# Overflow work of a third gathered in one place behind the upper projection, and the overflow tokens of the next expert transposed under a condition

## The chip, the cores and the metric

The kernel runs on one core of one Trainium2 chip. The metric is the device time in microseconds (us) of one execution. It was 2561.84 us before the change (median of 3 runs, 2560.95 to 2563.5). The granted TensorE clock of the profiled execution was 0.987 of full speed over the whole span.

## The reference, cut to what matters

The program is a cross attention, a self attention and a mixture of experts over 1024 tokens of 512 features. The change touches only the experts:

```python
NUM_EXPERTS, TOPK, FFN, CAPACITY = 64, 8, 1536, 160
gates = softmax(x @ wg.T); w_topk, idx_topk = top_k(gates, TOPK)      # 8 experts a token
# tokens sorted by expert; at most CAPACITY = 160 of them are kept for each expert
h = einsum('ech,efh->ecf', buf, expert_w1)       # gate and upper halves, 512 -> 2 x 1536
x1, x2 = split(h, 2)
out = einsum('ecf,ehf->ech', x1 * silu(x2), expert_w2)                # 1536 -> 512
result = x + shared_out + scatter_add(out * gate weight)
```

A mean expert gets 128 tokens (1024 x 8 / 64). Up to 160 count, so an expert has 128 regular tokens and up to 32 "overflow" tokens.

## The kernel before

**Tiling.** The 64 experts are worked off in order, each in three thirds of the hidden width (NB = 3, so n runs from 0 to 191; b = n % 3, e = n // 3). A third has three weight units of 1 MB: GATE, UPPER and DOWN. A unit lands in one of 10 slots (8 in `ring`, 2 in `e_more`). ScalarE rounds it to fp32r (`high`, line 1269, into e_WH), VectorE takes the rest (`low`, line 1348, into e_WL); both have 5 places (HELD), and a place is free again once TensorE has used the unit that was there. TensorE multiplies three times (high x high, high x low, low x high) for each of four slices, 12 matmuls of 128x512 a unit.

**The regular work of a third on TensorE**, in this order: `gates_of(n)` (12 matmuls, lines 1457 to 1459), `uppers_of(n)` (12, the same lines), `turn(n-1)` (4 fp32 transposes of the product of the third before, line 1507), `down(n-2)` (12 matmuls, lines 1535 to 1537).

**The overflow work.** The 32 overflow tokens are laid out as four column strips of 32: `over(n)` (line 1488) is 64 small fp32 matmuls with an output of 32x128, straight from the raw GATE and UPPER units; `over_turn(n-1)` (line 1498) is one fp32 transpose of 128x128; `over_down(n-2)` (line 1520) is 32 small matmuls from the raw DOWN unit. `narrow[e]` is 1 if expert e has at most 128 tokens and so no overflow; TensorE reads it into a register and skips `over` and `over_down` then. This text calls such an expert narrow, and the others wide. The overflow work stands in three places of a third: `over_turn` and `over` between `gates_of` and `uppers_of`, `over_down` between `turn` and `down`. With b = 0, `over_turn` runs outside the condition.

**The tokens of the next expert.** In the thirds with b = 1, between `gates_of` and `uppers_of`, `turn_tokens(e+1)` makes four fp32 transposes of the regular tokens (line 1445) and one of the overflow tokens (line 1448), always. It waits for the gather, for the copies out of the PSUM banks (`xel_done`, `xeo_done`), and, only ahead of the last transpose, for `gto_done`. ScalarE copies both out (lines 1299 and 1306), VectorE makes the low half (1370).

**The order on the other engines** is written out by hand and is the same for every third. ScalarE, step n: [b = 2: the weighing of the expert before, 1313 and 1314], `high(UPPER, n+1)`, `silu(n)` (1277), [b = 1: the token copies], `high(DOWN, n-1)`, `silu_over(n)` (1284), `high(GATE, n+2)`, `copy_turned(n-1)` (1291 and 1292). VectorE, step n: `low(UPPER, n+1)`, [b = 1: low tokens], `low(DOWN, n-1)`, `product(n)` (1356), `product_over(n)` (1363), `low(GATE, n+2)`, `turned_low(n-1)` (1376). Each of these runs for narrow experts too. SyncE's queue issues the loads (line 1257) in the order of use, each when the unit that was in its slot 10 loads earlier is used up: for GATE and UPPER of third n at `u_done` (the upper projection of n is done), for DOWN at `d_done`. GpSimd gathers tokens and adds results into DRAM.

Of the kernel before, what the change touches and what calls it, by code (L numbers as in the profile page):

```python
# [14 lines left out]
P = 128  # L15
# [4 lines left out]
G = D // P  # L20
# [3 lines left out]
NE = 64  # L24
# [91 lines left out]
def program(nc, x, ctx_k, ctx_v, wq, wk, wv, wo, bq, bk, bv, bo, wg, shared, experts, out):  # L116
    root = ExitStack()
    with root:
# [1070 lines left out]
        with ExitStack() as st:  # L1189
# [61 lines left out]
            @block.sync  # L1251
            def _(sp):
                for i in range(RING, 3 * NP):
                    if i >= R:
                        kind, n = ORDER[i - R]
                        sp.wait_ge(d_done if kind == DOWN else u_done, n + 1)
                    sp.dma_start(unit(i), source(i)).then_inc(unit_in[i % R], 16)

            @block.scalar
            def _(act):  # L1260
                def high(kind, n):

                    i = place(kind, n)
                    act.wait_ge(unit_in[i % R], 16 * (i // R + 1))
                    nth = NTH[kind, n]
                    if nth >= HELD:
                        was, m = SPLITS[nth - HELD]
                        act.wait_ge(consumed[was], m + 1)
                    act.activation(WH[:, nth % HELD, :], unit(i), ACT.Copy).then_inc(hi_done, 1)  # L1269

                def silu(n):
                    act.wait_ge(g_done, n + 1)
                    if n == 0:
                        act.wait_ge(so_out, 32)
                    if n >= 2:
                        act.wait_ge(gf_done, n - 1)
                    act.activation(SL[n % 2], gate_ps, ACT.Silu).then_inc(silu_done, 1)  # L1277

                def silu_over(n):

                    act.wait_ge(u_done, n + 1)
                    if n >= 1:
                        act.wait_ge(gfo_done, n)
                    act.activation(SLo[:, :], over_ps[:, 0:P], ACT.Silu).then_inc(slo_done, 1)  # L1284

                def copy_turned(n):

                    act.wait_ge(t_done, n + 1)
                    if n >= 2:
                        act.wait_ge(d_done, n - 1)  # L1290
                    act.activation(GTh[:, n % 2, :, :], turn_ps.rearrange("p (j n) -> p j n", j=G), ACT.Copy).then_inc(gt_done, 1)
                    act.activation(GTo[:, n % 2, :, :], overturn_ps.rearrange("p (j n) -> p j n", j=G), ACT.Copy).then_inc(gto_done, 1)

                def tokens_high(e):

                    act.wait_ge(xe_psum, e + 1)
                    if e >= 2:
                        act.wait_ge(u_done, NB * (e - 1))
                    act.activation(XEh[:, e % 2, :, :], token_ps.rearrange("p (k n) -> p k n", k=G), ACT.Copy).then_inc(xeh_done, 1)

                def tokens_over(e):

                    act.wait_ge(xe_psum, e + 1)
                    if e >= 2:
                        act.wait_ge(u_done, NB * (e - 1))
                    act.activation(XEo[:, e % 2, :, :], overtoken_ps.rearrange("p (k n) -> p k n", k=G), ACT.Copy).then_inc(xeo_done, 1)

                def weigh(e):

                    act.wait_ge(d_done, NB * e + NB)  # L1310
                    if e >= 1:
                        act.wait_ge(added, 32 * e)
                    act.activation(Y, down_ps, ACT.Copy, scale=gates[:, e, 0:1]).then_inc(y_ready, 1)
                    act.activation(Y2, overdown_ps, ACT.Copy, scale=gates[:, e, 1:2]).then_inc(y2_ready, 1)  # L1314

                high(GATE, 0)
                tokens_high(0)
                high(UPPER, 0)
                tokens_over(0)
                high(GATE, 1)  # L1320
                for n in range(NP):
                    e, b = n // NB, n % NB
                    if b == 2 and e >= 1:
                        weigh(e - 1)
                    if n + 1 < NP:
                        high(UPPER, n + 1)
                    silu(n)
                    if b == 1 and e + 1 < NE:
                        tokens_high(e + 1)
                        tokens_over(e + 1)  # L1330
                    if n >= 1:
                        high(DOWN, n - 1)
                    silu_over(n)
                    if n + 2 < NP:
                        high(GATE, n + 2)
                    if n >= 1:
                        copy_turned(n - 1)
                high(DOWN, NP - 1)
                copy_turned(NP - 1)
                weigh(NE - 1)  # L1340

            @block.vector
            def _(dve):
# [14 lines left out]
                def product_over(n):  # L1358

                    dve.wait_ge(slo_done, n + 1)  # L1360
                    if n >= 1:
                        dve.wait_ge(t_done, n)
                    dve.tensor_tensor(GFo[:, :], SLo[:, :], over_ps[:, P:2 * P], ALU.mult).then_inc(gfo_done, 1)

                def tokens_low(e):

                    dve.wait_ge(xeh_done, e + 1)
                    if e >= 2:
                        dve.wait_ge(u_done, NB * (e - 1))
                    dve.tensor_tensor(XEl[:, e % 2, :, :], token_ps.rearrange("p (k n) -> p k n", k=G), XEh[:, e % 2, :, :],  # L1370
                                      ALU.subtract).then_inc(xel_done, 1)
# [10 lines left out]
                low(GATE, 1)  # L1382
                for n in range(NP):
                    e, b = n // NB, n % NB
                    if n + 1 < NP:
                        low(UPPER, n + 1)
                    if b == 1 and e + 1 < NE:
                        tokens_low(e + 1)
                    if n >= 1:
                        low(DOWN, n - 1)  # L1390
                    product(n)
                    product_over(n)
                    if n + 2 < NP:
                        low(GATE, n + 2)
                    if n >= 1:
                        turned_low(n - 1)
                low(DOWN, NP - 1)
# [37 lines left out]

            @block.tensor
            def _(pe):
                def turn_tokens(e):

                    pe.wait_ge(gathered[e % 2], 32 * (e // 2 + 1))  # L1440
                    if e >= 1:
                        pe.wait_ge(xel_done, e)
                        pe.wait_ge(xeo_done, e)
                    for k in range(G):
                        pe.transpose(token_ps[:, k * P:(k + 1) * P], XG[:, e % 2, k * P:(k + 1) * P], ident[:, :])  # L1445
                    if e >= 2:
                        pe.wait_ge(gto_done, NB * (e - 1))
                    pe.transpose(overtoken_ps, XO[:, e % 2, :], ident[:, :]).then_inc(xe_psum, 1)  # L1448

                def project(dst, kind, n, done):  # L1450

# [18 lines left out]
                def uppers_of(n):  # L1470

                    if n >= 1:
                        pe.wait_ge(gf_done, n)
                    project(up_ps, UPPER, n, u_done)
# [17 lines left out]
                def over_turn(n):  # L1492

                    pe.wait_ge(gfo_done, n + 1)
                    if n >= 1:
                        pe.wait_ge(gto_done, n)
                    pe.wait_ge(xeo_done, min((n - 1) // NB + 2, NE))
                    pe.transpose(overturn_ps, GFo[:, :], ident[:, :])  # L1498

                def turn(n):  # L1500
# [36 lines left out]
                        last = pe.matmul(down_ps, l, wh, start=False, stop=(b == NB - 1 and j == G - 1))  # L1537
                    last.then_inc(d_done, 1)

                turn_tokens(0)  # L1540
                before = None
                for e in range(NE):
                    now = pe.value_load(narrow[0:1, e:e + 1], min_val=0, max_val=1)
                    for b in range(NB):
                        n = NB * e + b
                        gates_of(n)
                        if b == 0 and n >= 1:
                            over_turn(n - 1)
                        with pe.If(now < 1):
                            if b >= 1:  # L1550
                                over_turn(n - 1)
                            over(n)
                        if b == 1 and e + 1 < NE:
                            turn_tokens(e + 1)
                        uppers_of(n)
                        if n >= 1:
                            turn(n - 1)
                        if n >= 2:
                            with pe.If((now if b >= 2 else before) < 1):
                                over_down(n - 2)  # L1560
                            down(n - 2)
                    before = now
                over_turn(NP - 1)
# [63 lines left out]
```

## Time and profile before

| | |
|---|---|
| median of 3 runs | 2561.84 us (2560.95 to 2563.5) |
| profiled execution, own time | 2563.15 us |
| its span | 2561.4 us |
| PE (TensorE) busy | 2469.9 us, 96% |
| VectorE busy | 1982.8 us, 77% |
| ScalarE busy | 1674.0 us, 65% |
| GpSimd busy | 624.8 us, 24% |
| HBM over the span | 277 GB/s |
| the experts' part | from 601.6 us to the end |

Busy times are sums over the whole span; the first 600 us are the attentions, the routing and the shared expert. PE matmuls overlap in the profile (each is shown with 0.39 us but they start 0.23 us apart), so their starts have to be read, not their durations. "PEld" is TensorE's loading of the held operand.

### The profile page before, as it was taken

Reading aid. Unit: us, or ns where it says so; the run is one execution under the profiler, and the core shown is the slowest. Engines: PE = TensorE matmul, PEld = TensorE weight load, DVE = VectorE, ACT = ScalarE, POOL = GpSimd, SP = SyncE. Lnnn points to the kernel's source line nnn. Section 1 sums busy time; section 2 is a strip of 40 time slices with the busy share of each in tenths; the row PEclk is TensorE's granted clock in tenths of the full one; section 3 lists DMA queues with packets and bytes.
Section 4 is the critical chain, followed back from the end, with each engine's and each line's share of the span. In section 5 each row is a group of like instructions: output and inputs, shape, how many; then the busy total and the mean of one; then the engine's idle time right before and its main releaser. Section 6 shows DMA issues by size and latency. Waiting matters only on the chain.

```text
span 2561.4 us, 53432 instructions
## 1 busy us (share of the span) xinstructions
PE 2469.9 (96%) x21954; PEld 1969.7 (77%) x21954; DVE 1982.8 (77%) x1878; ACT 1674.0 (65%) x2107; POOL 624.8 (24%) x541
## 2 busy tenths in 40 slices
PE   6877989998999999999999999999999999999998
PEld 5763557776888888888888888888888888888886
DVE  6863457665799889998878988988778877867785
ACT  5641233334688788887767878877667767756774
POOL 3410020101233322422222332233212222222221
PEclk9988999998999999999999999999999999999999
DMA  6770022235899999999988999999889888877894
GB/s 202 221 218 0 2 108 106 97 153 197 288 381 384 343 351 384 378 377 328 355 300 317 365 347 353 384 349 346 291 304 322 319 299 314 323 282 269 317 361 131
DMA packets 128524, 714.96 MB, mean 279 GB/s; under 512 B 15488, under 2 KB 23808, under 8 KB 52416
## 3 DMA queue, kind: packets, MB, share of 16 engines
q1 hardware_dynamic: 102048, 665.96, 68.2%
q0 software_dynamic: 26144, 44.06, 8.6%
q8 instruction: 272, 4.46, 0.7%
q14 instruction: 60, 0.49, 0.1%
HBM read 684.46 MB, written 25.49 MB: 277 GB/s over the span
## 4 chain that ended last, share of the span: by engine, by line
PE 76%; DVE 0%; POOL 0%; issue 0%; ACT 0%; ACTq 0%; POOLq 0%; DVEq 0%
PE ps L1457 14%; PE ps L1459 14%; PE ps L1458 14%; PE ps L1535 7%; PE ps L1537 7%; PE ps L1536 7%; PE ps L1488 5%; PE ps L1507 3%; PE ps L1520 3%; PE ps L1445 1%; PE ps L1498 0%; PE ps L1448 0%; DVE e_WL L1348 0%; ACT e_WH L1269 0%; POOL out_rows L1419 0%
## 5 line engine op out<-in xcount | busy, mean ns | idle before, releaser
L1348 DVE TENSOR_TENSOR e_WL<-ring,e_WH 128x2048 fp32r<-128x2048 f32 x462 | 1057.3, 2289 | 227.7 <-ACT e_WH L1269 223.6
L1269 ACT ACTIVATE e_WH<-ring 128x2048 fp32r<-128x2048 f32 x462 | 883.5, 1913 | 115.8 <-PE ps L1537 98.8
L1457 PE MATMUL ps<-e_WH,e_XEh 128*128 128x512 f32 x1536 | 614.9, 400 | 3.6 <-DVE e_XEl L1370 3.6
L1459 PE MATMUL ps<-e_WH,e_XEl 128*128 128x512 f32 x1536 | 602.0, 392 | 0.0
L1458 PE MATMUL ps<-e_WL,e_XEh 128*128 128x512 f32 x1536 | 599.4, 390 | 0.0
L1407 POOL TENSOR_TENSOR e_tick<-e_tick 128x1 f32<-128x1 f32 x126 | 132.3, 1050 | 1337.8 <-ACT X L1314 1136.7
L1457 PEld LDWEIGHTS ps<-e_WH,e_XEh 128*128 128x128 f32 x1536 | 289.0, 188 | 72.3 <-issue 9.1
L1459 PEld LDWEIGHTS ps<-e_WH,e_XEl 128*128 128x128 f32 x1536 | 288.8, 188 | 62.8
L1458 PEld LDWEIGHTS ps<-e_WL,e_XEh 128*128 128x128 f32 x1536 | 289.4, 188 | 56.2
L1535 PE MATMUL ps<-e_WH,e_GTh 128*128 128x512 f32 x768 | 319.5, 416 | 0.4 <-issue 0.3
L1348 DVE TENSOR_TENSOR e_WL<-e_more,e_WH 128x2048 fp32r<-128x2048 f32 x114 | 260.8, 2289 | 53.9 <-ACT e_WH L1269 52.9
L1537 PE MATMUL ps<-e_WH,e_GTl 128*128 128x512 f32 x768 | 300.5, 391 | 0.0
L1536 PE MATMUL ps<-e_WL,e_GTh 128*128 128x512 f32 x768 | 299.9, 390 | 0.0
L1269 ACT ACTIVATE e_WH<-e_more 128x2048 fp32r<-128x2048 f32 x114 | 218.1, 1913 | 23.8 <-PE ps L1537 23.7
L1277 ACT ACTIVATE X<-ps 128x512 f32<-128x512 f32 x192 | 114.9, 599 | 97.6 <-PE ps L1459 97.6
L1535 PEld LDWEIGHTS ps<-e_WH,e_GTh 128*128 128x128 f32 x768 | 144.3, 188 | 39.1 <-issue 15.2
L1537 PEld LDWEIGHTS ps<-e_WH,e_GTl 128*128 128x128 f32 x768 | 144.2, 188 | 33.1
L1421 POOL DMA_INDIRECT out_rows<-X,lists x64 | 159.0, 2484 | 19.5 <-issue 19.5
L1536 PEld LDWEIGHTS ps<-e_WL,e_GTh 128*128 128x128 f32 x768 | 144.8, 189 | 24.2
L1284 ACT ACTIVATE e_SLo<-ps 128x128 f32<-128x128 f32 x192 | 53.2, 277 | 163.5 <-PE ps L1459 163.5
L1356 DVE TENSOR_TENSOR X<-X,ps 128x512 f32<-128x512 f32 x192 | 130.9, 682 | 15.8 <-PE ps L1459 15.8
L1376 DVE TENSOR_TENSOR e_GTl<-ps,e_GTh 128x512 fp32r<-128x512 f32 x192 | 131.1, 683 | 0.0
(207 smaller groups left out, 3269.7 us busy)
## 6 DMA issues: line engine op xcount, KB each, us to landing
ring<-in_experts SPq DMA_DIRECT2D x462, 1024.0 KB, 7.9
e_more<-in_experts SPq DMA_DIRECT2D x114, 1024.0 KB, 7.8
ring<-in_shared SPq DMA_DIRECT2D x12, 1536.0 KB, 6.3
a_K<-in_ctx_k SPq DMA_DIRECT2D x32, 514.0 KB, 5.2
a_V<-in_ctx_v SPq DMA_DIRECT2D x32, 384.0 KB
a_V<-in_ctx_v SPq DMA_DIRECT2D x32, 130.0 KB
X<-in_x SPq DMA_DIRECT2D x4, 512.0 KB, 5.3
xn_scratch<-ring SPq DMA_DIRECT2D x1, 2048.0 KB, 7.4
```

The source lines that it names most:

```text
L1269: act.activation(WH[:, nth % HELD, :], unit(i), ACT.Copy).then_inc(hi_done, 1)
L1348: dve.tensor_tensor(WL[:, at, :], unit(place(kind, n)), WH[:, at, :], ALU.subtract).then_inc(lo_done, 1)
L1356: dve.tensor_tensor(GF[n % 2], SL[n % 2], up_ps, ALU.mult).then_inc(gf_done, 1)
L1376: dve.tensor_tensor(GTl[:, n % 2, :, :], turn_ps.rearrange("p (j n) -> p j n", j=G), GTh[:, n % 2, :, :], ALU.subtract).then_inc(gtl_done, 1)
L1407: pool.tensor_tensor(tick[:, :], tick[:, :], tick[:, :], ALU.add).then_inc(ticked, 1)
L1421: pool.indirect_dma_start(out4, bass.IndirectOffsetOnAxis(lists[:, 1, e, 1:2], 0), Y2, None, compute_op=ALU.add).then_inc(added, 16)
L1457: pe.matmul(dst, h, wh, start=(k == 0), stop=False)
L1458: pe.matmul(dst, h, wl, start=False, stop=False)
L1459: last = pe.matmul(dst, l, wh, start=False, stop=(k == G - 1))
L1535: pe.matmul(down_ps, h, wh, start=(b == 0 and j == 0), stop=False)
L1536: pe.matmul(down_ps, h, wl, start=False, stop=False)
L1537: last = pe.matmul(down_ps, l, wh, start=False, stop=(b == NB - 1 and j == G - 1))
```

## The change

On TensorE, `turn_tokens(e+1)` moves to the start of the third (ahead of `gates_of`), the overflow transpose in it comes first and only if the next expert is wide. `over(n)`, `over_down(n-2)` and `over_turn(n-1)` stand together between `uppers_of(n)` and `turn(n-1)`, and all of them are conditional. The register for the next expert is read one expert ahead. The raw GATE and UPPER units are now read after `uppers_of`, so their slots are given back at `t_done` (the turn behind the overflow work) and not at `u_done`. On ScalarE and VectorE the token work goes to the start of the step, and `silu_over(n)` and `product_over(n)` behind the work on GATE of n+2; `silu_over` waits for `t_done`.

```diff
@@ block.sync
-                        sp.wait_ge(d_done if kind == DOWN else u_done, n + 1)
+                        if kind == DOWN:
+                            sp.wait_ge(d_done, n + 1)
+                        elif n >= 1:
+                            sp.wait_ge(t_done, n)
+                        else:
+                            sp.wait_ge(u_done, 1)
@@ block.scalar, silu_over
-                    act.wait_ge(u_done, n + 1)
+                    if n >= 1:
+                        act.wait_ge(t_done, n)
+                    else:
+                        act.wait_ge(u_done, 1)
@@ block.scalar, the steps
+                    if b == 1 and e + 1 < NE:
+                        tokens_high(e + 1)
+                        tokens_over(e + 1)
                     if n + 1 < NP:
                         high(UPPER, n + 1)
                     silu(n)
-                    if b == 1 and e + 1 < NE:
-                        tokens_high(e + 1)
-                        tokens_over(e + 1)
                     if n >= 1:
                         high(DOWN, n - 1)
-                    silu_over(n)
                     if n + 2 < NP:
                         high(GATE, n + 2)
+                    silu_over(n)
@@ block.vector, the steps
+                    if b == 1 and e + 1 < NE:
+                        tokens_low(e + 1)
                     if n + 1 < NP:
                         low(UPPER, n + 1)
-                    if b == 1 and e + 1 < NE:
-                        tokens_low(e + 1)
...
-                    product_over(n)
                     if n + 2 < NP:
                         low(GATE, n + 2)
+                    product_over(n)
@@ block.tensor, turn_tokens
-                    for k in range(G):
-                        pe.transpose(token_ps[:, k * P:(k + 1) * P], XG[:, e % 2, k * P:(k + 1) * P], ident[:, :])
                     if e >= 2:
                         pe.wait_ge(gto_done, NB * (e - 1))
-                    pe.transpose(overtoken_ps, XO[:, e % 2, :], ident[:, :]).then_inc(xe_psum, 1)
+                    with pe.If(alone < 1):
+                        pe.transpose(overtoken_ps, XO[:, e % 2, :], ident[:, :])
+                    for k in range(G):
+                        last = pe.transpose(token_ps[:, k * P:(k + 1) * P], XG[:, e % 2, k * P:(k + 1) * P], ident[:, :])
+                    last.then_inc(xe_psum, 1)
@@ block.tensor, over_turn
-                    pe.wait_ge(xeo_done, min((n - 1) // NB + 2, NE))
+                    pe.wait_ge(xeo_done, min(n // NB + 2, NE))
@@ block.tensor, the thirds
+                        if b == 1 and e + 1 < NE:
+                            turn_tokens(e + 1, after)
                         gates_of(n)
-                        if b == 0 and n >= 1:
-                            over_turn(n - 1)
-                        with pe.If(now < 1):
-                            if b >= 1:
-                                over_turn(n - 1)
-                            over(n)
-                        if b == 1 and e + 1 < NE:
-                            turn_tokens(e + 1)
+                        if n == 0:
+                            with pe.If(now < 1):
+                                over(n)
                         uppers_of(n)
+                        if b < 2 and n >= 2:
+                            with pe.If(before < 1):
+                                over_down(n - 2)
+                                if b == 0:
+                                    over_turn(n - 1)
                         if n >= 1:
+                            with pe.If(now < 1):
+                                over(n)
+                                if b == 2:
+                                    over_down(n - 2)
+                                if b >= 1:
+                                    over_turn(n - 1)
                             turn(n - 1)
                         if n >= 2:
-                            with pe.If((now if b >= 2 else before) < 1):
-                                over_down(n - 2)
                             down(n - 2)
```

## Rows read from the trace of the kernel before

**Rows 1.** The page: busy time by engine, and the chain that ended last.
```profile
PE 2469.9 (96%) x21954; PEld 1969.7 (77%) x21954; DVE 1982.8 (77%) x1878; ACT 1674.0 (65%) x2107; POOL 624.8 (24%) x541
...
PE 76%; DVE 0%; POOL 0%; issue 0%; ACT 0%; ACTq 0%; POOLq 0%; DVEq 0%
```

**Rows 2.** The waits of the whole span: us in total, times, longest.
```profile
PEld ps L1488 <- issue: 19.8, 68, 0.4
```

**Rows 3.** By line, count; ns min/median/max, first and last start.
```profile
L1488 PE MATMUL ps<-ring,e_XEo x3616: 272/273/298, 611.5 to 2505.7; 128*32 128x128 f32 x191
...
L1488 PE MATMUL ps<-e_more,e_XEo x800: 272/273/298, 640.9 to 2493.4; 128*32 128x128 f32 x160
...
L1498 PE MATMUL ps<-ident,e_GFo x110: 270/270/328, 619.1 to 2541.6; 128*128 128x128 f32 x110
...
L1448 PE MATMUL ps<-ident,XO x64: 272/272/421, 602.5 to 2495.0; 128*128 128x128 f32 x64
```

**Rows 4.** PE's timeline, two narrow thirds: start us, us, line, count.
```profile
809.63 0.39 PE L1457 MATMUL ps<-e_WH,e_XEh 128*128 128x512 f32 x1
...
812.35 0.27 PE L1498 MATMUL ps<-ident,e_GFo 128*128 128x128 f32 x1
...
815.23 0.60 PE L1507 MATMUL ps<-ident,X 128*128 128x128 f32 x4
...
818.43 0.39 PE L1457 MATMUL ps<-e_WH,e_XEh 128*128 128x512 f32 x1
...
821.16 0.60 PE L1445 MATMUL ps<-ident,XG 128*128 128x128 f32 x4
...
821.62 0.49 PE L1457 MATMUL ps<-e_WH,e_XEh 128*128 128x512 f32 x1
...
824.50 0.60 PE L1507 MATMUL ps<-ident,X 128*128 128x128 f32 x4
```

**Rows 5.** PE's timeline, a wide third: one transpose, over, upper projection, turn.
```profile
1504.05 0.27 PE L1498 MATMUL ps<-ident,e_GFo 128*128 128x128 f32 x1
1504.24 1.08 PE L1488 MATMUL ps<-ring,e_XEo 128*32 128x128 f32 x32
1505.14 1.06 PE L1488 MATMUL ps<-e_more,e_XEo 128*32 128x128 f32 x32
1506.13 0.50 PE L1457 MATMUL ps<-e_WH,e_XEh 128*128 128x512 f32 x1
...
1508.99 0.60 PE L1507 MATMUL ps<-ident,X 128*128 128x128 f32 x4
```

**Rows 6.** PE's timeline, over followed by the token transposes.
```profile
1515.12 1.96 PE L1488 MATMUL ps<-ring,e_XEo 128*32 128x128 f32 x64
1517.00 0.66 PE L1445 MATMUL ps<-ident,XG 128*128 128x128 f32 x4
...
1517.52 0.48 PE L1457 MATMUL ps<-e_WH,e_XEh 128*128 128x512 f32 x1
```

**Rows 7.** PE's timeline, turn, over_down and down.
```profile
1531.24 0.60 PE L1507 MATMUL ps<-ident,X 128*128 128x128 f32 x4
1531.77 1.08 PE L1520 MATMUL ps<-ring,e_GTo 128*32 128x128 f32 x32
1532.78 0.50 PE L1535 MATMUL ps<-e_WH,e_GTh 128*128 128x512 f32 x1
```

**Rows 8.** PEld's timeline behind a skipped over_down.
```profile
1119.56 0.19 PEld L1535 LDWEIGHTS ps<-e_WH,e_GTh 128*128 128x128 f32 x1 [0.34 <-issue]
```

**Rows 9.** ScalarE's timeline in the first narrow third of rows 4.
```profile
815.43 0.28 ACT L1284 ACTIVATE e_SLo<-ps 128x128 f32<-128x128 f32 x1 [0.47 <-PE ps L1459]
...
817.88 0.28 ACT L1292 ACTIVATE e_GTo<-ps 128x128 f32<-128x128 f32 x1
```

**Rows 10.** The loads at line 1257, and a stretch of narrow experts (busy us, clock, DMA share, GB/s).
```profile
DMA to landing us min/median/max: 4.6/7.9/12.3
...
716.00:860.00 144.00, 144.00 (x681) 118.70 (x680) 134.15 (x104) 122.98 (x135) 49.04 (x33) 1.00 1.01 382
```

More of the change, by code:

```diff
@@ L1437, in _, with turn_tokens @@
             def _(pe):
-                def turn_tokens(e):
+                def turn_tokens(e, alone):
                     pe.wait_ge(gathered[e % 2], 32 * (e // 2 + 1))
@@ L1538, in down @@
                     last.then_inc(d_done, 1)
-                turn_tokens(0)
-                before = None
+                now = pe.value_load(narrow[0:1, 0:1], min_val=0, max_val=1)
+                turn_tokens(0, now)
+                before = after = None
                 for e in range(NE):
-                    now = pe.value_load(narrow[0:1, e:e + 1], min_val=0, max_val=1)
+                    if e >= 1:
+                        now = after
+                    if e + 1 < NE:
+                        after = pe.value_load(narrow[0:1, e + 1:e + 2], min_val=0, max_val=1)
                     for b in range(NB):
                         n = NB * e + b
+                        if b == 1 and e + 1 < NE:
+                            turn_tokens(e + 1, after)
                         gates_of(n)
-                        if b == 0 and n >= 1:
-                            over_turn(n - 1)
-                        with pe.If(now < 1):
-                            if b >= 1:
-                                over_turn(n - 1)
-                            over(n)
-                        if b == 1 and e + 1 < NE:
-                            turn_tokens(e + 1)
-                        uppers_of(n)
-                        if n >= 1:
+                        if n == 0:
+                            with pe.If(now < 1):
+                                over(n)
+                        uppers_of(n)
+                        if b < 2 and n >= 2:
[3 more added lines that the diff above has]
+                                    over_turn(n - 1)
+                        if n >= 1:
+                            with pe.If(now < 1):
[4 more added lines that the diff above has]
+                                    over_turn(n - 1)
                             turn(n - 1)
                         if n >= 2:
-                            with pe.If((now if b >= 2 else before) < 1):
-                                over_down(n - 2)
                             down(n - 2)
```

## The prediction

> **What bounds the kernel now.** I read the page first: PE is busy 96% of the span and holds 76% of the chain that ended last, with nothing from another engine above 0% [rows 1]. Then the waits: of TensorE's there is hardly one for another engine; what remains is "issue", such as 19.8 us ahead of the overflow loads [rows 2]. Then PE's timeline, third by third, by starts, since shown durations overlap. The expert part is a train without holes: 12 matmuls of 512 columns take 2.72 to 2.73 us (809.63 to 812.35 [rows 4]), and the other engines run behind with idle time of their own. So the time is the sum of what TensorE issues, and the change is priced there; the other engines count only where the new order makes TensorE wait.
>
> **Prices on TensorE.**
> - A regular block of 12: 2.725 us.
> - A turn and the down block behind it: 815.23 to 818.43, 3.20 us [rows 4]. With 2.725 for the block that leaves .475 for four transposes, some .107 each and .04 for the return to big matmuls. One transpose alone (over_turn of a narrow expert, skipped over behind it) costs 815.23 - 812.35 - 2.725 = .155 [rows 4].
> - Five token transposes alone, 821.16 to 821.62, .46, and the block behind 2.88: .61 in all [rows 4].
> - 32 small matmuls: .90 (1504.24 to 1505.14) [rows 5].
> - Going into the small ones: transpose to over 1504.05 to 1504.24, .19 instead of .107, so .09 [rows 5]; four transposes to over_down .53 instead of .43, so .10 [rows 7]. Take .10. An entry straight from a big matmul isn't in these rows; between 0 and .25 (a whole matmul pitch), I take .10.
> - Leaving them: the second 32 take .99 and the block behind 2.86 instead of 2.725, so .22 into big matmuls [rows 5]. Into transposes: over takes 1.88 (.08 more than 1.80) and the five cost .52 instead of .46 [rows 6], so .14.
>
> So each excursion into the small matmuls costs .24 to .32 us besides its work. Why: PEld sits idle with "issue" 68 times, a total of 19.8 us, just ahead of line 1488 [rows 2], which is .29 each; the first small load doesn't begin under the matmul before it, as other loads do. The Trainium skill, TensorEngine Tiling (Array Packing), Key Properties, says that changing the tiling mode, not merely the tile, drains the engine; by that rule two runs of the same mode back to back pay once. The rows have no over beside an over_down, so that they merge is what I infer: between free (the ring half and the e_more half of rows 5 stand .90 apart) and the full .32. I take free, since both use the same 128x32 form.
>
> **How often.** Line 1488 ran 3616 + 800 = 4416 times [rows 3], 64 a third: 69 thirds, 23 wide experts, 41 narrow ones. Line 1498 ran 110 times: 46 within wide experts, 64 outside any condition [rows 3]. By the timeline the wide ones are 0, 1, 9, 19, 23, 24, 26, 31, 38, 41, 42, 43, 45, 47, 49, 50, 52, 54 to 58 and 62. Of the 63 boundaries 9 are wide-wide, 13 narrow-wide, 14 wide-narrow, 27 narrow-narrow.
>
> **The sum, by kind of third** (base without extras: three blocks 8.175 + .475 = 8.65; entry .10, exit into transposes .14):
> - b = 2, wide. Before: .19 + 1.89 + .135 for transpose, over and exit, .10 + .90 + .235 for over_down (its .11 tail and .125 in the down block): 12.10, read as 12.06. After: 8.65 + .10 + 2.70 + .14 + .107 = 11.70. Saves .36 x 23 = 8.3.
> - b = 0, wide-wide: over_down and over_turn in one condition, over in the next, so two excursions: 8.65 + .10 + .90 + .14 + .107 + .10 + 1.80 + .14 = 11.94 against 12.06. Saves .12 x 9 = 1.1.
> - b = 0, narrow-wide: 10.69 against 10.87; the transpose of the dead overflow goes: .18 x 13 = 2.3.
> - b = 0, wide-narrow: 9.90 against 9.97: .07 x 14 = 1.0.
> - b = 0, narrow-narrow: 8.65 against 8.80 (809.63 to 818.43 [rows 4]): .155 x 27 = 4.2.
> - b = 1: the token transposes cost .61 at their new place; before, behind over, they shared its exit. Wide-wide: 8.65 + .61 + .10 + 2.70 + .14 + .107 = 12.31 against 12.60, .29 x 9 = 2.6. Narrow-wide 11.40 against 11.38: nothing. Wide-narrow 10.39 against 10.43: .04 x 13 = .5. Narrow-narrow: nothing.
> - The conditional overflow transpose: .107 saved for each of the 41 narrow experts among the 64 that line 1448 now serves [rows 3]: 4.4.
>
> Together 24.4 us, all of it on the path. Ends: if an entry from a big matmul is free, .10 less on some 23 + 31 + 36 excursions, 9 more; if it costs .25, 13 less; if over and over_down don't merge, .24 to .32 less on 32 thirds, 8 to 10 less.
>
> The number of conditions stays about equal (six an expert) with one more for the token transpose. Skipped ones cost nothing today: a narrow third without extras is the bare sum, 8.64.
>
> **The other engines.** Raw slots of GATE and UPPER come free at the turn: .4 us later in a narrow third, up to 3.4 later in a wide one (over and over_down 2.7, entry and exit, turn). Behind that wait SyncE's queue holds the next loads, DOWN's too. Measured from the turn the tightest is UPPER: issued at the turn of n-2, needed by ScalarE's `high` at the end of `down` in third n-1, 2.85 + 8.65 = 11.5 us later. Loads land in 7.9 us, at most 12.3 [rows 10]; a late one has about .7 us before silu's own wait (ScalarE sits idle between them) and a third until TensorE wants it. So it is covered, by not much in narrow stretches. There the loads already run at a DMA share of 1.01 and 382 GB/s over 144 us [rows 10], without falling behind; the change asks for about 1.5% more.
>
> Token work first delays `high(UPPER, n+1)` by about 1 us; it waits for the end of `down` anyway, and its product is wanted a third later. The late `silu_over` and `product_over` have the next upper block, over 5 us, before over needs them.
>
> One new chain is narrow. Token transposes now stand at the start of b = 1 and wait for `gto_done` up front. In a narrow b = 0 third ScalarE gets from the end of `uppers_of` to the end of copy 1292 in 815.43 to 818.16, 2.73 us [rows 9]; the order of the pieces changes, not their sum. TensorE needs 3.20 for turn and down [rows 4], and the last upper matmul ends .16 behind the turn's start, .20 with the signal. That leaves 3.20 - .20 - 2.73 = .27, less the .23 by which a load leads its matmul: about zero. Between 0 and .2 us, 27 times: 0 to 5 us. I take .03, 1 us.
>
> So 24.4 - 1 = 23.4 us from the profiled execution's 2563.15: 2539.8. The median shown is 1.3 lower: 2538.5, rounded 2538.
>
> **Rivals.**
> 1. *The feed becomes the bound in narrow stretches* (loads or the ScalarE chain). For: share 1.01, landings up to 12.3, and the chain above with no slack. Against: nothing falls behind in the 144 us of rows 10, and no wait of ScalarE for a load shows. Then narrow thirds stay as they are: 4.2 and three quarters of 4.4 are lost, 2546.
> 2. *No merging*: the cost of an excursion goes with every change of destination, not of form. Some 10 lost: 2548.
> 3. *Skipping costs, and the kernel gets slower.* Now skips stand between gates and uppers and between turn and down. In three narrow thirds a skipped over_down left a hole with nothing to wait for, .34 us at 1119.56 [rows 8], the three together 1.15 us. The change puts both skips side by side ahead of the turn, so that narrow experts jump over some 190 instructions at once. If each of the roughly 150 thirds with a skip paid .38, that is 57 us, 24 saved, so 2562 + 33 = 2595; it decides from about 65 such holes. Against: behind big matmuls (the over skip today) no hole shows in 42 thirds, and the new place is of that kind. The Trainium skill, Runtime: NRT & Kernel Launch, Instruction fetch mechanics, says that a taken branch whose target is outside the fetched window stalls until it is fetched; the three holes would fit, and the other hundred or more skips say that it seldom happens.
> 4. *The conditional parts don't do what they say* (narrow experts few, or transposes hidden): nothing saved but b = 2. Rows 3 speak against it. 2554 to 2560.
>
> **How the numbers follow.** Forecast 2538, chance .66 (own range 2532 to 2544); feed .13, 2546; no merging .09, 2548; skips .07, mostly 2570 to 2595 but a few holes would be 2545; nothing much .05, 2558. What a measurement of this kernel can tell is about 0.2%, 5 us: faster means under 2556.7. Faster .86, same .06, slower .08. Range 2530 to 2551: it takes in the cheaper entry at the low end (9 less, of which I believe half at most) and rivals 1 and 2 at the high end.
>
> **What would show it.** Wide b = 2 thirds of 11.7 (from 12.06), with one "issue" idle of PEld ahead of line 1488 and none ahead of 1520 in them; narrow thirds with b = 0 of 8.64; line 1448 23 times, the over_turn line 70; token transposes with no wait for ScalarE. It is wrong if PE waits for copy 1292 or for fetched weights, if over to over_down costs more than .03, or if there are "issue" holes behind skips.

## The result: less than half of what was forecast

| | before | changed |
|---|---|---|
| median | 2562.36 us (6 runs) | 2552.19 us (6 runs, 2547.24 to 2554.93) |
| ratio, 95% interval | | 0.9958 [0.9945, 0.997] |
| profiled execution, own time | 2563.15 | 2553.26 |
| its span | 2561.4 | 2551.5 |
| first gates block starts | 606.47 | 610.53 |
| from there to TensorE's last matmul | 1944.2 | 1930.4 |
| the 188 thirds n = 3 to 190 | 1895.8 | 1882.4 |

The change is faster by .42%, some 11 us; the forecast was 24 less, 2538, with a range of 2530 to 2551, so the result, 2552.19, lies just outside it. In this pair of traces the expert part gained 13.8 us, and the part ahead of it, whose code is the same, lost 4.1. I come back to these 4 us below.

The page of the changed kernel, busy time and chain, against [rows 1]:
```profile
PE 2451.1 (96%) x21873; PEld 1958.6 (77%) x21873; DVE 1977.8 (78%) x1878; ACT 1678.5 (66%) x2107; POOL 637.0 (25%) x541
...
PE 75%; issue 0%; DVE 0%; POOL 0%; ACT 0%; ACTq 0%; POOLq 0%; DVEq 0%
```
TensorE still sets the time, and its busy time fell by 18.8 us. In the changed kernel, transposes of the overflow tokens and over_turn, as in [rows 3] (count; ns min/median/max):
```profile
L1455 PE MATMUL ps<-ident,XO x23: 270/272/465, 606.8 to 2451.9; 128*128 128x128 f32 x23
...
L1508 PE MATMUL ps<-ident,e_GFo x70: 270/328/331, 628.4 to 2531.8; 128*128 128x128 f32 x70
```
23 for 64 and 70 for 110, as forecast. A wide third with b = 2 on PE's timeline (start us, us), which answers to [rows 5, 7]:
```profile
664.83 0.39 PE L1467 MATMUL ps<-e_WH,e_XEh 128*128 128x512 f32 x1
...
670.36 1.95 PE L1498 MATMUL ps<-ring,e_XEo 128*32 128x128 f32 x64
672.13 1.06 PE L1530 MATMUL ps<-ring,e_GTo 128*32 128x128 f32 x32
673.12 0.33 PE L1508 MATMUL ps<-ident,e_GFo 128*128 128x128 f32 x1
673.29 0.60 PE L1517 MATMUL ps<-ident,X 128*128 128x128 f32 x4
...
676.49 0.39 PE L1467 MATMUL ps<-e_WH,e_XEh 128*128 128x512 f32 x1
```
664.83 to 676.49 is 11.66 us, forecast 11.70, before 12.06. Over begins 1.77 us ahead of over_down and not 1.89, so there is no exit between them. So far all is as priced. Now a narrow third with b = 0, where nothing should stand but 8.65 us of regular work; PE, PEld and ScalarE in the changed kernel, three views in turn, against [rows 4, 9]:
```profile
732.00 0.39 PE L1467 MATMUL ps<-e_WH,e_XEh 128*128 128x512 f32 x1
...
740.42 0.39 PE L1547 MATMUL ps<-e_WH,e_GTl 128*128 128x512 f32 x1
740.86 0.66 PE L1457 MATMUL ps<-ident,XG 128*128 128x128 f32 x4
```
```profile
740.86 0.42 PEld L1457 LDWEIGHTS ps<-ident,XG 128*128 128x128 f32 x4 [0.47 <-issue]
```
```profile
737.71 1.92 ACT L1274 ACTIVATE e_WH<-ring 128x2048 fp32r<-128x2048 f32 x1 [0.38 <-PE ps L1469]
739.53 0.26 ACT L1292 ACTIVATE e_SLo<-ps 128x128 f32<-128x128 f32 x1
739.68 0.60 ACT L1299 ACTIVATE e_GTh<-ps 128x512 fp32r<-128x512 f32 x1
740.16 0.29 ACT L1300 ACTIVATE e_GTo<-ps 128x128 f32<-128x128 f32 x1
```
The token transposes begin at 740.86, .44 behind the last matmul of down, which is .21 more than a matmul's distance. ScalarE's copy, on which `gto_done` hangs, ends at 740.45, so the load could have followed almost at once; .41 us lie between them. What stands in between is in the records of the branch of the token condition, which is TensorE's own queue (count; ns; start):
```profile
L1454 PEldq COMPARE_BRANCH  x1: 217/217/217, 740.6 to 740.6; - x1
```
TensorE's queue, which otherwise runs well ahead of the array (the branch ahead of the next turn runs at 743.2, the turn at 746.85), stood at the wait until 740.5, and only then did the branch behind the wait run. Of the 27 narrow-narrow b = 0 thirds 7 take about 8.70, 18 take 8.85 and two 8.99; altogether they cost 4.7 us more than 27 x 8.65.

And one third later, in the same expert (e = 4), PE's timeline:
```profile
746.85 0.60 PE L1517 MATMUL ps<-ident,X 128*128 128x128 f32 x4
747.20 0.48 PE L1545 MATMUL ps<-e_WH,e_GTh 128*128 128x512 f32 x1
748.88 0.39 PE L1546 MATMUL ps<-e_WL,e_GTh 128*128 128x512 f32 x1 [1.20 <-issue]
```
A hole of 1.4 us with nothing to wait for, between the first and the second matmul of `down`. There are five, all at this place, in experts 4, 12, 28, 36 and 60: 7.5 us together. These are all the narrow experts behind a narrow one whose number divided by 8 leaves 4. Before, there were three in other places, 1.2 us together [rows 8].

### The profile page after: what moved, and what is told of

The parts are those of the page before. It is cut to its first block, busy times and chain, and to the rows that moved or that the text cites. A ratio compares the mean times of both kernels' runs of the same rounds, so it can differ in the third digit from the quotient of the medians.

```text
span 2551.5 us, 53292 instructions
## 1 busy us (share of the span) xinstructions
PE 2451.1 (96%) x21873; PEld 1958.6 (77%) x21873; DVE 1977.8 (78%) x1878; ACT 1678.5 (66%) x2107; POOL 637.0 (25%) x541
## 4 chain that ended last, share of the span: by engine, by line
PE 75%; issue 0%; DVE 0%; POOL 0%; ACT 0%; ACTq 0%; POOLq 0%; DVEq 0%
PE ps L1467 14%; PE ps L1469 14%; PE ps L1468 14%; PE ps L1545 7%; PE ps L1547 7%; PE ps L1546 7%; PE ps L1498 5%; PE ps L1517 4%; PE ps L1530 3%; PE ps L1457 1%; PE ps L1508 1%; PE ps L1455 0%; DVE e_WL L1356 0%; ACT e_WH L1274 0%; POOL out_rows L1427 0%
## 5 line engine op out<-in xcount | busy, mean ns | idle before, releaser
L1467 PE MATMUL ps<-e_WH,e_XEh 128*128 128x512 f32 x1536 | 605.2, 394 | 2.4 <-DVE e_XEl L1378 2.4
L1415 POOL TENSOR_TENSOR e_tick<-e_tick 128x1 f32<-128x1 f32 x126 | 113.5, 901 | 1308.0 <-ACT X L1322 1211.8
L1429 POOL DMA_INDIRECT out_rows<-X,lists x64 | 174.4, 2725 | 19.5 <-issue 19.5
L670 POOL DMA_INDIRECT XO<-xn_scratch,lists x64 | 127.4, 1991 | 19.5 <-issue 18.6
```

What stands on the lines that cost most here:

```text
L1429: pool.indirect_dma_start(out4, bass.IndirectOffsetOnAxis(lists[:, 1, e, 1:2], 0), Y2, None, compute_op=ALU.add).then_inc(added, 16)
L1467: pe.matmul(dst, h, wh, start=(k == 0), stop=False)
```

## The experiments

Every run is timed against the kernel before on its own chip. The table comes from each one's trace: the expert part runs from the first gates block to the last matmul; "b = 0" is the usual length of a narrow-narrow third with b = 0; a hole is what a third takes over the shortest of its kind, from .2 us on, waits of the b = 0 thirds left out.

| kernel | ratio to before [95%] | expert part | 188 thirds | b = 0 | holes |
|---|---|---|---|---|---|
| before | 1 | 1944.2 | 1895.8 | 8.80 | 3, 1.2 us |
| changed | 0.9958 [0.9945, 0.997] | 1930.4 | 1882.4 | 8.85 | 5, 7.5 us |
| changed, again | 0.9948 [0.9934, 0.9962] | 1930.3 | 1882.0 | 8.85 | 5, 7.0 us |
| wait in the condition | 0.9898 [0.9882, 0.9914] | 1918.3 | 1870.2 | 8.65 | 2, 1.2 us |
| no conditions | 0.9895 [0.9878, 0.9911] | 1916.3 | 1868.9 | 8.65 | none |
| copies first on ScalarE | 0.9887 [0.9871, 0.9904] | 1917.2 | 1868.8 | 8.65 | none |
| wait behind the condition | 0.9901 [0.9885, 0.9918] | 1920.8 | 1872.7 | 8.65 | 4, 4.0 us |
| shifted by 64 | one run, no interval | 1925.4 | 1879.7 | 8.85 | 4, 4.4 us |
| over_down put back | 0.9987 [0.9977, 0.9997] | 1940.8 | 1892.4 | 8.85 | 3, 4.8 us |
| only the conditional transpose | 0.9979 [0.9968, 0.999] | 1939.3 | 1890.9 | 8.79 | 2, 1.1 us |
| over_turn behind over, b = 0 | 0.9879 [0.9862, 0.9895] | 1915.1 | 1867.8 | 8.65 | 1, 1.4 us |
| both best parts | 0.9886 [0.987, 0.9902] | 1914.4 | 1866.3 | 8.65 | none |

**The wait inside the condition.**
```diff
-                    if e >= 2:
-                        pe.wait_ge(gto_done, NB * (e - 1))
                     with pe.If(alone < 1):
+                        if e >= 2:
+                            pe.wait_ge(gto_done, NB * (e - 1))
                         pe.transpose(overtoken_ps, XO[:, e % 2, :], ident[:, :])
```


> The changed kernel, but TensorE's wait for gto_done stands inside the condition, so it is waited for only where the overflow transpose runs. Theory A (the b = 0 narrow thirds of 8.86 us are token transposes that wait for the copy at line 1300 and then for the branch behind that wait): these 22 thirds fall to 8.65, 4 to 5 us less than the changed kernel, ratio to before about 0.994. Rival B (it is the branch itself, or the wait for the low tokens): they stay at 8.86. The fetch holes of 1 to 1.6 us behind skips stay in either case, at other experts perhaps, since the code shifts by one or two instructions an expert.

Measured 2538.46 us, ratio 0.9898: 12 us less in the expert part than the changed kernel, not 4 to 5. The b = 0 thirds fell to 8.65 as theory A has it, and the five holes went as well, which I had not expected of this kernel. Two of .84 and .34 stand elsewhere, in experts 18 and 61, whose next expert is wide, so there the wait is still carried out. But this edit moves the code a little too, so it can't tell by itself why the holes went.

**No conditions at run time.** `pe.If(...)` becomes Python's `if` with the list of the wide experts; the wait ahead of the token transposes stays where the change has it.

> The changed kernel with no condition at run time: the overflow instructions are emitted for the 23 wide experts alone, which are listed in the program for these inputs. Theory A (the five holes of 1.0 to 1.6 us in the down block of narrow b = 1 thirds are instruction fetch behind skipped code): none is left, 7 us less than the changed kernel, and the token transposes behind the wait lose the branch too, 2 to 4 us of their 5; together 9 to 11 less, some 2541 us. Rival C (the holes are transfers or the profile itself): they stay, and only the branch's part goes, 2 to 4 us. Rival D (every skip costs a little that hides in the pitch): all thirds get shorter, more than 15 us less.

Measured 2539.27 us, 0.9895, 14.1 us less in the expert part than the changed kernel (9 to 11 were expected). No hole is left, and apart from the narrow-narrow thirds no kind got shorter: wide b = 2 thirds take 11.66 in both. So rivals C and D fall; in these thirds a skip costs nothing. And the b = 0 thirds are 8.65 with the wait for `gto_done` in its place. So the wait as such costs nothing; the .2 us need the branch behind it.

**Only the conditional transpose, in the kernel before.** `turn_tokens` as in the change, but left behind `gates_of`.

> The kernel before with one part of the change: the overflow tokens are transposed under a condition, first, in the old place behind gates_of; all else as before. By the prediction's price 41 x .107 = 4.4 us less than before, ratio .998. Here the wait for gto_done comes a gates block later, so it should be over long before and no branch is exposed. Rival: behind the wait the branch costs as much as the transpose saves; then no change, or 63 x .2 us more.

Measured 2559.98 us against 2565.74, ratio 0.9979: 4.9 us less in the expert part and in the thirds, 4.4 forecast. Narrow thirds with b = 1 and a narrow expert next take 9.13 instead of 9.25, where the price says .107.

**over_down back between turn and down.**
```diff
-                        if b < 2 and n >= 2:
+                        if b == 0 and n >= 2:
                             with pe.If(before < 1):
-                                over_down(n - 2)
                                 if b == 0:
                                     over_turn(n - 1)
...
                                 over(n)
-                                if b == 2:
-                                    over_down(n - 2)
...
                         if n >= 2:
+                            with pe.If((now if b >= 2 else before) < 1):
+                                over_down(n - 2)
                             down(n - 2)
```


> The changed kernel with over_down put back between turn and down, under its own condition; over, over_turn and the token work as changed. Theory A (an excursion into the small matmuls costs .24 to .32 us, and over and over_down share one when they stand together): 23 thirds with b = 2 and 9 with b = 1 cost .3 more, 8 to 10 us; the two skips don't stand side by side any more, so the holes fall from 7 us to about 1, as before the change. Net 2 to 4 us more than the changed kernel. Rival B (no merging): no third gets longer, 6 us less than the changed kernel. Rival C (the holes have nothing to do with neighbouring skips): 8 to 10 us more.

Measured 2562.8 us, 0.9987, 10.4 us more in the expert part than the changed kernel. One wide b = 2 third on PE's timeline:
```profile
667.91 1.95 PE L1498 MATMUL ps<-ring,e_XEo 128*32 128x128 f32 x64
669.80 0.33 PE L1508 MATMUL ps<-ident,e_GFo 128*128 128x128 f32 x1
669.96 0.60 PE L1517 MATMUL ps<-ident,X 128*128 128x128 f32 x4
670.49 1.08 PE L1530 MATMUL ps<-ring,e_GTo 128*32 128x128 f32 x32
671.50 0.50 PE L1545 MATMUL ps<-e_WH,e_GTh 128*128 128x512 f32 x1
```
Over to the first transpose 1.89 (1.77 when over_down follows), turn to over_down .53: both prices of an excursion are paid twice. These thirds take 12.00 instead of 11.66, and the 9 wide-wide ones with b = 1 take .34 more too. The merging is shown, and is worth 32 x .34 = 10.9 us. The holes did not fall to 1 us: 2.0, 1.6 and 1.2, all in b = 1 thirds, whose skips no longer stand side by side. So a hole needs no neighbouring skips, and the total came out as rival C has it.

**Copies first on ScalarE.** This one decides between the wait and the place of the code, since TensorE's program is the changed kernel's.
```diff
-                    if n + 2 < NP:
-                        high(GATE, n + 2)
                     silu_over(n)
                     if n >= 1:
                         copy_turned(n - 1)
+                    if n + 2 < NP:
+                        high(GATE, n + 2)
```


> The changed kernel with one swap on ScalarE: silu_over and copy_turned come ahead of the work on GATE of n+2. TensorE's code is the changed kernel's to the instruction. Then gto_done comes about 1.2 us behind the turn, long before the token transposes ask. Theory A (TensorE's queue is stopped at the wait with a branch behind it, so the branch is exposed, and the lead that hides the fetch of the next code block is lost): b = 0 narrow thirds 8.65, no hole of 1 us or more in experts 4, 12, 28, 36 and 60; some 12 us less than the changed kernel, like the kernel with the wait inside the condition. Rival B (the holes come from where the code falls in its 16 KB blocks, which repeats every 8 experts, and the wait has no part in them): thirds 8.65, but the five holes stay: 5 us less only. Rival C (late GATE work on ScalarE and VectorE makes TensorE wait for the low part): new idle time ahead of gates_of, no gain.

Measured 2538.18 us, 0.9887, 13.2 us less in the expert part. Theory A. ScalarE and PE in this kernel around the same token transposes of expert 5, and the same branch:
```profile
741.02 0.59 ACT L1299 ACTIVATE e_GTh<-ps 128x512 fp32r<-128x512 f32 x1
741.50 0.29 ACT L1300 ACTIVATE e_GTo<-ps 128x128 f32<-128x128 f32 x1
```
```profile
743.19 0.39 PE L1547 MATMUL ps<-e_WH,e_GTl 128*128 128x512 f32 x1
743.43 0.60 PE L1457 MATMUL ps<-ident,XG 128*128 128x128 f32 x4
```
```profile
L1454 PEldq COMPARE_BRANCH  x1: 217/217/217, 741.9 to 741.9; - x1
```
The copy ends at 741.79, the branch runs at 741.9, 1.5 us before the transposes begin (.26 before, in the changed kernel), and they follow the last matmul by .24. All 27 thirds take 8.65 to 8.66, and not one of the 188 shows a hole. TensorE's code and the data are the same; what differs is ScalarE's order, and so when its copies and what hangs on them are done. Rival C doesn't show: the late GATE work costs nothing.

The place of the code still shows in TensorE's queue. These are its waits ahead of `down` (line 1539) and behind it (1463) in the b = 1 third of expert 4, first in the changed kernel, then in this one:
```profile
L1539 PEldq EVENT_SEMAPHORE  x1: 51/51/51, 743.7 to 743.7; - x1
L1463 PEldq EVENT_SEMAPHORE  x1: 51/51/51, 748.9 to 748.9; - x1
```
```profile
L1539 PEldq EVENT_SEMAPHORE  x1: 51/51/51, 746.9 to 746.9; - x1
L1463 PEldq EVENT_SEMAPHORE  x1: 51/51/51, 749.2 to 749.2; - x1
```
The changed kernel's queue needs 5.0 to 5.5 us for this stretch in the five experts with a hole and 2.7 in most other narrow-narrow thirds with b = 1. With the copies first it needs 2.3 to 2.7 in the same five and 2.0 in most others. So the queue is held up in the same places in both kernels, but much shorter here, and the array doesn't feel it.

**The wait behind the condition.**
```diff
                     with pe.If(alone < 1):
+                        if e >= 2:
+                            pe.wait_ge(gto_done, NB * (e - 1))
                         pe.transpose(overtoken_ps, XO[:, e % 2, :], ident[:, :])
+                    if e >= 2:
+                        pe.wait_ge(gto_done, NB * (e - 1))
```


> The changed kernel with the wait for gto_done inside the condition and once more behind it, ahead of the four token transposes: TensorE still stops there in narrow thirds, but no branch stands right behind the wait. Theory A1 (the .15 to .34 us are the branch that can't be run ahead of the wait): thirds of 8.65 with b = 0. Theory A2 (it is the wait itself that comes late): they stay at 8.80 to 8.86. On the holes: if the stop as such eats the lead that covers a code fetch, holes of 1 us or more appear again, at other experts; if a branch behind the stop is needed, none. 2538 to 2548 us.

Measured 2541.64 us, 0.9901. A1: 8.65, though TensorE stops as late as in the changed kernel. And there are four holes, 4.0 us: .97, .25, .58 and this one, PE's timeline, of an ordinary b = 0 third:
```profile
1665.42 0.39 PE L1471 MATMUL ps<-e_WH,e_XEl 128*128 128x512 f32 x1
1667.78 0.41 PE L1519 MATMUL ps<-ident,X 128*128 128x128 f32 x2 [1.97 <-issue]
```
So a branch right behind the stop is needed for the .2 us. For the holes this run shows only that the branch isn't needed: three of them stand in b = 1 thirds, but the one above stands in expert 37 with b = 0, two thirds behind the last such wait.

**Code shifted.**
```diff
+                pe.wait_ge(gathered[0], 32)
+                for _ in range(64):
+                    pe.transpose(overtoken_ps, XO[:, 0, :], ident[:, :])
                 turn_tokens(0, now)
```


> The changed kernel with 64 more transposes of 128x128 into the overflow tokens' PSUM bank ahead of the expert part (some 7 us, partly under the wait for the first weights), which shifts all later code of TensorE by 64 matmuls and loads. Theory A (fetch of code blocks): the holes of the down block leave experts 4, 12, 28, 36 and 60 and turn up, if at all, in other experts or at other places of the third; the b = 0 narrow thirds stay at 8.86. Rival (holes from transfers of weights, or from the data of those experts): the same five experts.

The holes left experts 4, 12, 28, 36 and 60 and stand in 8, 11, 16 and 40 (1.64, .97, 1.40 and .38 us). The first and the third stand at the old place in `down`, that of expert 11 ahead of the turn, that of 40 ahead of the turn of its b = 2 third. In expert 8, PE's timeline:
```profile
861.32 0.39 PE L1546 MATMUL ps<-e_WL,e_GTh 128*128 128x512 f32 x1 [1.48 <-issue]
```
The b = 0 thirds stayed at 8.85. Experts 8, 16 and 40 are all the narrow ones behind a narrow one whose number divides by 8. So the place of the code decides where a hole falls, not the data or the loads of those experts.

**The changed kernel again.**

> The changed kernel once more, on the chip of these comparisons. If the holes are where the code falls in its blocks together with the late wait, they stand in experts 4, 12, 28, 36 and 60 again, the b = 0 narrow thirds take 8.86 again, and the ratio is 0.995 to 0.996. If they are chance, they stand elsewhere. The start of the first gates block (606.5 us before, 610.5 after in the first pair of traces) tells whether the 4 us ahead of the expert part belong to the changed program or to the execution.

Measured 2553.3 us, 0.9948 [0.9934, 0.9962], and the five holes in the same five experts (two of them on PE's timeline):
```profile
748.10 0.39 PE L1546 MATMUL ps<-e_WL,e_GTh 128*128 128x512 f32 x1 [1.21 <-issue]
```
```profile
972.20 0.39 PE L1546 MATMUL ps<-e_WL,e_GTh 128*128 128x512 f32 x1 [1.22 <-issue]
```
They are not chance. The first gates block began at 609.5.

**over_turn behind over.** On the kernel with the wait inside the condition, in b = 0 thirds: `If(before)`: over_down; `If(now)`: over; `If(before)`: over_turn.

> The kernel with the wait inside the condition, and over_turn of the b = 0 thirds in a condition of its own behind over, so that over_down and over stand side by side there too. By the price of an excursion (.24 to .34 us) the 9 wide-wide thirds with b = 0 fall from 11.95 to 11.65 to 11.7, 2 to 3 us less than the kernel with the wait inside, ratio about 0.989. Rival: the third condition in a row costs more than that: skips stand three in a row in 27 narrow-narrow thirds, whose length of 8.65 would grow, or more fetch holes show; then no gain or some us more.

Measured 2536.43 us, 0.9879. The wide-wide b = 0 thirds fell from 11.95 to 11.67, PE's timeline of one:
```profile
1293.14 1.08 PE L1530 MATMUL ps<-ring,e_GTo 128*32 128x128 f32 x32
1294.04 1.93 PE L1498 MATMUL ps<-ring,e_XEo 128*32 128x128 f32 x64
1295.90 0.33 PE L1508 MATMUL ps<-ident,e_GFo 128*128 128x128 f32 x1
```
.90 from one to the other, as within one of them, though a condition lies between. Three skips in a row left the 27 narrow-narrow thirds at 8.65. One hole of 1.4 us stands in expert 28, at the old place in `down` (PE's timeline):
```profile
1431.07 0.39 PE L1546 MATMUL ps<-e_WL,e_GTh 128*128 128x512 f32 x1 [1.21 <-issue]
```
Expert 29 is narrow, so in that third the wait for `gto_done` is skipped: a hole doesn't need that wait.

**Both best parts**, the last kernel with the copies first on ScalarE.

> The kernel with the wait inside the condition and over_turn behind over in b = 0 thirds, and besides ScalarE's copies ahead of the work on GATE of n+2. Each part as measured alone: narrow thirds 8.65, wide-wide b = 0 thirds 11.67, and since nothing makes TensorE's queue stop in the narrow thirds, no fetch hole: 1.5 us less in the expert part than without the new order on ScalarE, 29 less than the kernel before, ratio 0.988. Rival: three skips in a row make holes of their own, and they stay (1 to 3 us).

Measured 2534.45 us, 0.9886 [0.987, 0.9902]. In the expert part it is the shortest, 29.8 us less than before and 16 less than the changed kernel, with no hole: against the last kernel only ScalarE's order differs, and the hole of expert 28 is gone. Its ratio can't be told from those of its two parts alone, but is clear of the changed kernel's, on the same chip 0.9948.

## Why the prediction was wrong

**The sum of prices was right.** With copies first, and so without the late wait and the holes, the 188 thirds take 1868.8 us, 27.0 less than before. Forecast were 24.4, and 1.2 more go because the holes of before went; the rest is spread over the kinds. By kind: b = 2 wide 12.06 to 11.66 (forecast 11.70); b = 0 wide-wide 11.95 (11.94), narrow-wide 10.68 (10.69), wide-narrow 9.92 (9.90), narrow-narrow 8.65; b = 1 wide-wide 12.24 (12.31). What I inferred without a row held: over and over_down stand together with no exit between them, and an entry straight from a big matmul costs .09 (2.81 for the block ahead of it against 2.725). The Trainium skill, TensorEngine Tiling (Array Packing), Key Properties, says that a change of the tiling mode drains the engine; the .34 us of a split pair and the .90 from one run to the next agree.

**The failed steps are "One new chain is narrow", sized "0 to 5 us, I take .03, 1 us", and the holes, which stand in the sum at nothing.** The changed kernel gives back 13.6 of the 27.0 us, all of it in narrow-narrow thirds: 4.7 with b = 0, 1.4 in b = 1 around the token transposes, and 7.5 as holes in b = 1. The chain was to cost 1 us and cost 6.1. Its timing was right: ScalarE's 2.73 us against TensorE's 3.2 leave nothing, and where no branch follows (no conditions; wait behind) TensorE indeed loses nothing. I had counted only when the signal comes, not what stands in TensorE's queue behind the wait: a branch, which can be run ahead only if the queue gets past the wait. It showed as .2 us in most b = 0 thirds and .05 to .34 in all. This cause is shown.

The larger part is the 7.5 us of holes. The prediction has them only in rival 3, and its sum says that skipped conditions cost nothing. Two things are shown. Where a hole falls hangs on the place of the code (the same five experts twice, others when the code is shifted). And with ScalarE's copies first there is none, in two kernels (one trace each) that differ in nothing else from kernels with holes: copies first against changed, both best parts against over_turn behind over. All nine traces with conditions and late copies, the kernel before among them, have 1 to 5 holes. That the wait for `gto_done` is what turns a late copy into a hole isn't shown: most holes went when it moved into the condition, but there is a hole in expert 28 of over_turn behind over, where it is skipped, and one in expert 37 of the wait behind, two thirds away from it.

**Rival 3 had the right kind of event and the wrong cause.** It put holes on skips that stand side by side, .38 us each. They are 1.1 to 1.7 us in the changed kernel, only five, all with the skips side by side; but with skips side by side and the copies first there is none, and with the skips of the b = 1 thirds apart there are three (over_down put back). For a few holes it named 2545, well inside the range, and gave all of rival 3 a chance of .07. The Trainium skill, Runtime: NRT & Kernel Launch, Instruction fetch mechanics, describes code that arrives in 16 KiB blocks, and a stall where a branch leaves the fetched window. Holes without a releaser that move with the code and vanish without conditions agree with it, but that a fetch is what TensorE stood for is inferred: the instruction queue's records don't tell whose block they carry. Nor did a run show how late copies lead to a hole; in the changed kernel the later branches of that third ran about as far ahead of the array as with the copies first, and only then, between the waits of lines 1539 and 1463, was the queue held up for longer.

**Rivals 1, 2 and 4 fall.** The loads took 8.3 us for 7.9 in the median, and no engine waited for one. Merging is .34 us, 32 times. The conditional parts do what they say.

**The 4 us ahead of the expert part.** The first gates block began at 606.5 before, 610.5 and 609.5 in the two traces of the changed kernel, and between 606.7 and 613.1 in those of the experiments, whose code up to there is the same; copies first has 613.1 and the kernel closest to it, both best parts, 607.0. So it goes with the execution or with how a program lies, not with the change. What sets it is open. It is most of why one profiled span says 9.9 us and the expert part 13.8; the two ratios say 11 and 13. Taken from 2561.84, the gain of the expert part alone would give 2548, inside the range: it would have been luck, for the chain and the holes were just as wrong.

## What to carry to other kernels

On an engine whose queue runs ahead, price a wait by what stands behind it in the queue, not only by when its signal comes: a wait that is over "just in time" cost nothing in front of a matmul here, but exposed a branch. Where code is skipped at run time, look for holes with no releaser too, and see whether they go when the signals that TensorE waits for come earlier; here they did. Put a wait that only a conditional instruction needs inside the condition, or let the releasing engine do that copy before its long work. When small matmuls of another tile form have to be mixed in, put all of a stage's in one run, also across conditions.

## What the runs showed of the hardware

- A skipped condition cost TensorE nothing while its queue was ahead, holes apart: narrow-narrow thirds with b = 0 take 8.65 us with conditions and without, with up to three skips in a row.
- A compare-and-branch of TensorE's queue took 217 ns in the row above, and showed as time of the third, mostly .2 us, only right behind a late wait.
- Between two runs of 128x32 matmuls there is no gap (.90 us for each 32), between these and 128x128 work .09 to .10 on the way in and .14 to .22 on the way out; .34 us in all where a pair is split.
- Holes of 1.1 to 1.7 us without a releaser came back in the same five experts in two executions, and moved to others when 64 matmuls were put ahead. There TensorE's queue took some 2.5 us longer than elsewhere (5.0 to 5.5 us for a stretch of 2.7).
